# A first stage in another order: one block of a transformer on one NeuronCore

## What is computed

```
mod = silu(c) @ wmod                      # six sections: sa, ca, ga, sb, cb, gb for each batch
h   = layernorm(x) * (1 + ca) + sa
x   = x + ga * attn(h)                    # Mamba2-like: in_proj, causal conv of 4 taps, silu,
                                          # chunked scan with decays, gate silu(z), out_proj
h   = layernorm(x) * (1 + cb) + sb
x   = x + gb * (h @ (sign(w) * mean|w|).T + bias)
```

## Time and profile before

| | us |
|---|---|
| median of 3 executions | 655.74 (654.91 to 656.59) |
| the profiled execution | 658.04 |
| its span in the profile | 656.3 |
| TensorE busy | 612.0 (93%) |
| VectorE busy | 504.1 (77%) |
| ScalarE busy | 383.8 (58%) |
| GpSimd busy | 355.8 (54%) |

### The profile page before, as it was taken

One profiled execution on the slowest core, in us unless ns is written; L12 is line 12 of the kernel. 1 busy time (PEld: TensorE's weight loads), 2 busy tenths in 40 slices (PEclk: granted clock), 3 DMA queues, 4 the chain that ended last, 5 costly groups with the idle time before them and its releaser, 6 DMA issues.

```text
span 656.3 us, 21241 instructions
## 1 busy us (share of the span) xinstructions
PE 612.0 (93%) x8345; PEld 481.2 (73%) x8345; DVE 504.1 (77%) x928; ACT 383.8 (58%) x844; POOL 355.8 (54%) x411
## 2 busy tenths in 40 slices
PE   2788899999999999999999999999997999999995
PEld 1565677787787777878777787787875777888884
DVE  6797799978778787787977778778695566787756
ACT  2788555456465455655545655656664437566565
POOL 4776114347537355554543755547574657766642
PEclk9799999999999999999999999999999999999999
DMA  8734120613221221421222253231325735444411
GB/s 296 224 131 163 39 67 29 203 66 103 67 92 60 83 72 54 148 74 41 70 76 100 88 152 102 70 120 64 97 71 166 224 106 147 137 129 128 129 49 64
DMA packets 59866, 70.52 MB, mean 107 GB/s; under 512 B 13972, under 2 KB 33460, under 8 KB 59256
## 3 DMA queue, kind: packets, MB, share of 16 engines
q1 hardware_dynamic: 59768, 69.17, 33.0%
HBM read 54.45 MB, written 14.70 MB: 105 GB/s over the span
## 4 chain that ended last, share of the span: by engine, by line
PE 78%; DVE 7%; POOL 4%; issue 4%; ACT 3%; DMA 3%; SPq 1%; POOLq 0%; DVEq 0%; ACTq 0%
PE bank L1218 37%; PE bank L1985 12%; PE pair L1283 7%; PE bank L1227 4%; PE bank L2018 4%; PE pair L1256 3%; PE bank L1313 2%; PE bank L1236 2%; PE pair L1269 2%; DVE m_cv L1472 1%; POOL h_lo L435 1%; PE pair L1296 1%; DMA h_lo_place<-y_scratch 1%; PE bank L1245 1%; DVE p_xn L514 1%
## 5 line engine op out<-in xcount | busy, mean ns | idle before, releaser
L1472 DVE SCALAR_TENSOR_TENSOR m_cv<-bank,gpc,m_cv 128x511 f32<-128x511 f32 (+2 forms) x192 | 143.5, 748 | 36.0 <-ACT m_cv L1375 31.5
L1218 PE MATMUL bank<-h_hi,w_hi 128*128 128x512 f32 x384 | 163.2, 425 | 1.6 <-POOL h_lo L435 1.5
L1218 PE MATMUL bank<-h_hi,w_lo 128*128 128x512 f32 x384 | 152.0, 396 | 0.0
L1218 PE MATMUL bank<-h_lo,w_hi 128*128 128x512 f32 x384 | 151.4, 394 | 0.0
L1387 ACT ACTIVATE m_M<-bank 128x512 f32<-128x512 f32 x128 | 76.1, 594 | 65.9 <-PE bank L1227 64.1
L1375 ACT ACTIVATE m_cv<-bank,gpc 128x512 f32<-128x512 f32 x96 | 72.0, 750 | 72.6 <-PE bank L1218 72.1
L1614 POOL TENSOR_TENSOR m_S<-m_S,m_cd 128x128 f32<-128x128 f32 x96 | 40.2, 419 | 126.5 <-DVE m_S L1535 65.4
L1218 PEld LDWEIGHTS bank<-h_hi,w_hi 128*128 128x128 f32 x384 | 73.1, 190 | 22.1 <-issue 3.1
L1604 POOL TENSOR_TENSOR m_Xw<-m_Xp,wend 128x256 f32<-128x256 f32 x64 | 39.8, 622 | 85.4 <-ACT m_Xp L1395 85.4
L1218 PEld LDWEIGHTS bank<-h_hi,w_lo 128*128 128x128 f32 x384 | 72.5, 189 | 16.7
L1502 DVE TENSOR_TENSOR m_M<-m_M,pair 128x512 f32<-128x512 f32 x128 | 81.8, 680 | 0.3 <-issue 0.3
(11 more groups left out here) (179 smaller groups left out, 1228.9 us busy)
## 6 DMA issues: line engine op xcount, KB each, us to landing
m_ea<-ea_scratch SPq DMA_DIRECT2D x32, 256.0 KB
m_dd<-dd_scratch SPq DMA_DIRECT2D x32, 256.0 KB
y_scratch<-m_t SPq DMA_DIRECT2D x16, 512.0 KB, 3.4
h_lo_place<-y_scratch SPq DMA_DIRECT2D x16, 512.0 KB, 4.5
p_wm<-in_L_wmod_dram SPq DMA_DIRECT2D x6, 1024.0 KB, 6.7
m_wraw<-in_L_attn_in_proj_w_dram SPq DMA_DIRECT2D x18, 256.0 KB, 3.4
w_lo_place<-in_L_attn_input__dram SPq DMA_DIRECT2D x16, 256.0 KB, 4.8
out_dram<-t_o SPq DMA_DIRECT2D x16, 256.0 KB, 2.3
```

The source lines that it names most:

```text
L1218: ins = pe.matmul(A[k % 3][:, :], w[:, t, kc, :], h[:, n % NB, kc, :], start=(m == 0), stop=(m == 11))
L1472: ins = dve.scalar_tensor_tensor(out=cv[:, k % 3, lag:], in0=A[k % 3][:, 0:L - lag], scalar=s.gpc[:, gp, o:o + 1], in1=cv[:, k % 3, lag:], ...
```

## The change

It does four things.
- **Order in the first part.** VectorE does the product for silu(c), two `statistics`, the scaled copy for `mod`, two more `statistics`, and only then the memsets of the constant shapes. The two memsets of `wa_hi` and `wa_lo` go to GpSimd. GpSimd does `roots(0)` before `constant_shapes`, and `roots(3)` behind `low_part(6)`. TensorE does four turns before `early_sections` and the `wa` transposes; `late_sections(k)` each stand one project later, and `turn(12)` to `turn(15)` ahead of `late_sections(2)`. VectorE does `low_part(5)` and `low_part(7)` before `normalize(8)`, and `normalize(12)` to `normalize(15)` before `low_sums`. ScalarE does `decays` and `tanh(0)` ahead of `linear(2)`, and `copy_rows(1)` behind `linear(3)`.
- **Constant shapes by DMA.** The four copies of `stage` and `lstage` into `s.R` and `s.Lm` are issued by SyncE, ahead of the loads of x tiles 8 to 13, and no longer done by ScalarE.
- **dt_inputs(1, 0)** stands at the very end of TensorE's first part.
- **The last pair's step inputs.** `dt_inputs(1, 1)` stands at v = -2, sl = 3, in front of the second decay product; `softplus_inputs(1)` is cut in two, and its first two activations stand at v = -2, sl = 3, in front of ScalarE's other work of that slot; the gate transposes and gate rows stand in the same slot, and only their wait (`gates_turned`) at v = -1, sl = 0.

The diff, cut to its core:

```diff
@@ sync
         load_small()
+        sp.wait_ge(konst, 9)
+        for i in range(2):
+            sp.dma_start(s.R[:, i, :, :].bitcast(F32).rearrange("p q n -> p (q n)"), stage[:, :]).then_inc(kcopy, 16)
+            sp.dma_start(s.Lm[:, i, :, :].bitcast(F32).rearrange("p q n -> p (q n)"), lstage[:, :]).then_inc(kcopy, 16)
         for i in range(8, 14):
             load_x(i)
@@ gpsimd
+        pool.memset(wa_hi[:, :, :].bitcast(F32), 0.0).then_inc(zero_sc, 1)
+        pool.memset(wa_lo[:, :, :].bitcast(F32), 0.0).then_inc(zero_sc, 1)
...
+        roots(0)
         constant_shapes()
-        pool.wait_ge(konst, 9)
-        roots(0)
         chunk_starts()
...
         weights(1)
-        roots(3)
         low_part(4)
         low_part(6)
+        roots(3)
@@ vector
         dve.wait_ge(cond_step, 3)
+        for i in range(2):
+            statistics(dve, i)
         dve.wait_ge(zero_sc, 1)
...
-        for i in range(4):
+        for i in range(2, 4):
             statistics(dve, i)
+        for i, (first, _) in enumerate(LOG1P):
+            ins = dve.memset(root[:, i:i + 1], first)
+        ins.then_inc(a_root, 1)
+        dve.memset(stage[:, :], 0.0)
+        dve.memset(lstage[0:64, :], 0.0)
+        dve.memset(lstage[64:R_ALL, :], 1.0)
+        dve.memset(chunk_on[:, :], 1.0).then_inc(gpc_half, 1)
         for i in range(4):
             normalize(i)
...
-        normalize(8)
         low_part(5)
         low_part(7)
-        normalize(9)
-        normalize(10)
-        normalize(11)
+        for i in range(8, 12):
+            normalize(i)
...
         sums(dve, 0)
-        normalize(12)
+        for i in range(12, 16):
+            normalize(i)
         low_sums(dve, 0)
-        for i in range(13, 16):
-            normalize(i)
@@ scalar (first part)
         linear(1)
+        decays(act, 0)
+        tanh(0)
         linear(2)
-        decays(act, 0)
-        copy_rows(1)
         make_h(12)
         make_h(13)
-        tanh(0)
         make_h(14)
         make_h(15)
         tanh(1)
         linear(3)
+        copy_rows(1)
         tanh(2)
@@ gate_rows
-        softplus_inputs(act, 1)
         act.wait_ge(gate_pe, 1)
         act.activation(grow[:, :], MOD[0:2 * NB * KC, 0:P], ACT.Copy).then_inc(gate_ready, 1)
+        softplus_powers(act, 1)
         squares(act, 1, range(0, 2))
@@ tensor (first part)
         pe.wait_ge(cond_step, 4)
-        turn(0)
-        turn(1)
+        for i in range(4):
+            turn(i)
+        early_sections()
...
-        late_sections(0)
         project(1, 0)
         project(1, 1)
-        late_sections(1)
+        late_sections(0)
         project(2, 0)
         project(2, 1)
-        late_sections(2)
-        late_sections(3)
+        late_sections(1)
         for i in range(12, 16):
             turn(i)
-        dt_inputs(pe, 1, 0)
+        late_sections(2)
         project(3, 0)
         project(3, 1)
+        late_sections(3)
         pe.wait_ge(h_act, 14)
         end_turn(pe, 0)
+        dt_inputs(pe, 1, 0)
@@ tensor (main loop)
+                    if (v, sl) == (-2, 3):
+                        start.dt_inputs(pe, 1, 1)
                     if (v, sl) == (-1, 0):
-                        start.dt_inputs(pe, 1, 1)
-                        start.gate_turn(pe)
+                        start.gates_turned(pe)
...
                         turn_b(u)
+                    if (v, sl) == (-2, 3):
+                        start.gate_turn(pe)
@@ scalar (main loop)
-                    if (v, sl) == (-1, 0):
-                        start.gate_rows(act)
+                    if (v, sl) == (-2, 3):
+                        start.softplus_inputs(act, 1)
                     if slot >= 1 and piece_at(slot - 1) is not None:
                         weights(piece_at(slot - 1))
...
                         copy_b(u)
+                    if (v, sl) == (-2, 3):
+                        start.gate_rows(act)
```

More of the change, by code:

```diff
@@ L484, in vector @@
     def vector(dve, convolve, silu):
-        for i, (first, _) in enumerate(LOG1P):
-            ins = dve.memset(root[:, i:i + 1], first)
-        ins.then_inc(a_root, 1)
-        dve.memset(wa_hi[:, :, :].bitcast(F32), 0.0)
-        dve.memset(wa_lo[:, :, :].bitcast(F32), 0.0)
-        dve.memset(stage[:, :], 0.0)
-        dve.memset(lstage[0:64, :], 0.0)
-        dve.memset(lstage[64:R_ALL, :], 1.0)
-        dve.memset(chunk_on[:, :], 1.0).then_inc(gpc_half, 1)
         dve.wait_ge(d_c, 16)
@@ L522, in low_part @@
                               ALU.subtract).then_inc(h_lo[1], 1)
-        for i in range(4):
+        for i in range(2, 4):
             statistics(dve, i)
+        for i, (first, _) in enumerate(LOG1P):
[5 more added lines that the diff above has]
+        dve.memset(chunk_on[:, :], 1.0).then_inc(gpc_half, 1)
         for i in range(4):
             normalize(i)
-        dve.wait_ge(gpc_half, 1)
-        dve.wait_ge(wa_act, 1)
-        dve.tensor_tensor(wa_lo[:, :, 64:128], s.bank[5][:, 0:KC * NH].rearrange("p (k h) -> p k h", k=KC),
-                          wa_hi[:, :, 64:128].bitcast(F32), ALU.subtract).then_inc(wa_dve, 1)
         for i in range(4, 7):
@@ L535, in vector @@
         modulation(1)
+        dve.wait_ge(zero_sc, 3)
+        dve.wait_ge(wa_act, 1)
+        dve.tensor_tensor(wa_lo[:, :, 64:128], s.bank[5][:, 0:KC * NH].rearrange("p (k h) -> p k h", k=KC),
+                          wa_hi[:, :, 64:128].bitcast(F32), ALU.subtract).then_inc(wa_dve, 1)
         normalize(4)
@@ L659, in softplus_inputs, with softplus_powers @@
         act.activation(s.chain[:, pb, 1, :], DTB[:, :], ACT.Abs).then_inc(a_exp[pb], 1)
+    def softplus_powers(act, pb):
         act.wait_ge(a_exp[pb], 2)
@@ L703, in copy_rows @@
             act.activation(row[:, late, cols], DTB[:, cols], ACT.Copy).then_inc(sec_cp, 1)
-        act.wait_ge(konst, 9)
-        for i in range(2):
-            act.activation(s.R[:, i, :, :].rearrange("p q n -> p (q n)"), stage[:, :], ACT.Copy).then_inc(kcopy, 1)
-            act.activation(s.Lm[:, i, :, :].rearrange("p q n -> p (q n)"), lstage[:, :], ACT.Copy).then_inc(kcopy, 1)
+        copy_rows(0)
         act.wait_ge(wa_pe, 1)
+        act.wait_ge(zero_sc, 3)
         act.activation(wa_hi[:, :, 64:128], s.bank[5][:, 0:KC * NH].rearrange("p (k h) -> p k h", k=KC), ACT.Copy).then_inc(wa_act, 1)
-        copy_rows(0)
         for n in range(4):
@@ L720, in scalar @@
         softplus_inputs(act, 0)
+        softplus_powers(act, 0)
         squares(act, 0, range(5))
@@ L872, in tensor @@
         ins.then_inc(wa_pe, 1)
-        early_sections()
-        turn(2)
-        turn(3)
         turn_rows(pe, 0)
@@ L898, in tensor @@
             turn(i)
-        late_sections(0)
         project(1, 0)
         project(1, 1)
-        late_sections(1)
+        late_sections(0)
         project(2, 0)
         project(2, 1)
-        late_sections(2)
-        late_sections(3)
+        late_sections(1)
         for i in range(12, 16):
             turn(i)
-        dt_inputs(pe, 1, 0)
+        late_sections(2)
         project(3, 0)
         project(3, 1)
+        late_sections(3)
         pe.wait_ge(h_act, 14)
         end_turn(pe, 0)
+        dt_inputs(pe, 1, 0)
     start.sync, start.tensor, start.scalar, start.vector, start.gpsimd = sync, tensor, scalar, vector, gpsimd
     start.store_decays, start.store_skips, start.store_gates = store_decays, store_skips, store_gates
-    start.factors, start.finish_times, start.sums, start.low_sums, start.skips, start.squares = factors, finish_times, sums, low_sums, skips, squares
+    start.factors, start.finish_times, start.sums, start.low_sums, start.skips, start.squares, start.softplus_inputs = factors, finish_times, sums, low_sums, skips, squares, softplus_inputs
     start.decays, start.end_copy, start.end_turn = decays, end_copy, end_turn
-    start.gate_turn, start.gate_rows, start.gate_values, start.wait_low = gate_turn, gate_rows, gate_values, wait_low
+    start.gate_turn, start.gate_rows, start.gate_values, start.wait_low, start.gates_turned = gate_turn, gate_rows, gate_values, wait_low, gates_turned
     start.turn_sections, start.dt_inputs, start.gate_sizes, start.mlp_columns = turn_sections, dt_inputs, gate_sizes, mlp_columns
@@ L1132, in sync @@
             start.sync(sp)
-            sp.wait_ge(start.kcopy, 4)
+            sp.wait_ge(start.kcopy, 64)
             start.store_decays(sp, 0)
```

3 lines of the change are left out of this document (2 added, 1 removed).

## The result

| | us |
|---|---|
| kernel before, median | 655.71 (654.91 to 656.59) |
| kernel after, median | 665.34 (660.47 to 666.42) |
| ratio, with its 95% interval | 1.0121 (1.0088 to 1.0154) |
| profiled execution of after, its span | 660.47, 658.6 |

The change makes the kernel 9.6 us slower. The forecast was 660.6 and its range ended at 663.0. The profiled execution happens to be the quickest of the four; the other three took 665.3 to 666.4. So this profile can be laid beside the forecast step by step, but it holds only part of the loss; a second profile, shown with the first experiment, holds the rest.

A forecast was written before the change was run, and what follows sets the result against it. VectorE was taken as the bound from about 80 to 129 us. `convolve(4)` 6.5 us late less 1.2 slack gave 5.3; small gaps take about 0.3; +4.9 was taken: 655.74 + 4.9 = 660.6 us, range 654.8 to 663.0.

The forecast's parts named there:

- the deciding step: 61 to 91 us: softplus pair ahead of `linear(4)` makes `convolve(4)` 6.5 us late; 5.3 left at 86.14 after 1.2 slack.
- the middle: 49 to 63 us: four `normalize`s fill VectorE's wait, ending about 54.9; `silu(0)` ends at 60.7, 1.8 us sooner.
- the clock: `project(3)`, after TensorE idles from about 56.5 to 60.85 us: lower granted clock loses 1.7 us, bounds 0 and 3.0.
- `normalize` 0 to 3: VectorE's front: first starts about 10.4 us beside the `affine_select`s, fourth ends at 14.1; bounds 12.65 and 16.2.
- the term of the DMA copies: Four copies ahead of x8 to x13: 0 to 0.9 us of waiting for weight blocks, taken as 0.
- The issue: SyncE's four copy issues take 2.01 us; all later loads shift 2 to 2.4 us.
- The x tiles: x8 to x11 have one to two microseconds between landing and reading.
- The cover: TensorE's idle time of 1.53 us at 45.45 hides the weight-block wait; without it 0.9 us.
- the front order: 0 to 41 us: `factors(0)` comes at 40.8 instead of 41.21; bounds 39.3 and 42.2.
- Same: Rival, chance 0.17: TensorE's own order decides, `states(0)` +1.6 us, saved clock dip -1.7; 655.7 us.
- faster: Rival, chance 0.07: unhindered `normalize`s, clock stays up, VectorE's lateness within slack, `linear(4)` before 72.5; 652.1 us.
- Slower still: Rival, chance 0.08: TensorE, waiting for VectorE's mixes between 85 and 105 us, drops clock; another 1.7 to 3 us: 663.

The follow-up runs named there:

- the first experiment: The changed kernel run again without any edit, with a second profile and more executions (after_again): median 665.95 us, +8.9 over before.
- pair_behind: Changed kernel with the two softplus activations moved behind `linear(4)`, `exponent(0, 1)` and `copy_b` on ScalarE: median 661.38 us, +4.3 over before.
- slot_only: Kernel before with only the last pair's step inputs a slot earlier, softplus pair in front of `linear(4)`: median 659.02 us, +2.1.
- mid_only: Kernel before with only the change's middle (48 to 70 us), including `dt_inputs(1, 0)` at the end of the first part: median 659.99 us, +3.2.
- hole_slot: Kernel before with `skips(0)` moved into VectorE's wait for `decays`, and last pair's inputs a slot earlier, softplus pair behind `linear(4)`: 654.95 us, -2.0.
- dma_only: Kernel before with only the four constant-shape copies made DMAs ahead of x tile 8 instead of ScalarE activations: median 661.08 us, +4.2.
- copies_late: Changed kernel with the four constant-shape copies issued behind SyncE's loads of the first part: median 661.86 us, +4.9 over before.
- after_again: The changed kernel, no edit, profiled a second time with more executions: median 665.95 us, +8.9 over before.

## Why the prediction was right and where it failed

**Right: what bounds the kernel, and the deciding step.** VectorE's work between 80 and 129 us sets the time at which TensorE reaches its closed stretch. The forecast had `linear(4)` at 77.95 and `convolve(4)` 6.5 us late; measured 78.32 and 7.03. The reciprocal was to end at 84.5 and ends at 84.7. The lateness handed on was to be 5.3 us at the `convolve` of 86.14; it is 5.6 there and 5.6 at unit 6 in the first profile, and 5.3 to 5.5 at unit 6 in all three profiles with this order once the front is taken off. That this is the softplus pair and the queue behind `project(3)` is shown by pair_behind, slot_only and mid_only.

**Right: the middle and the clock.** `low_sums` starts at 55.70, where 54.9 was taken and 55.2 was the upper bound (0.65 us of it is that `factors(0)` came at 41.45 instead of 40.8); `silu(0)` starts at 60.74 and ends near 61.4 instead of 60.7. The four `normalize`s take 5.76 us, 1.44 each: each as long as one beside GpSimd in the row of before (1.45), and none was quicker. The granted clock of 60:66 is 0.72, which is the dip of the earlier trace rows moved: 1.7 us, as forecast, and `project(3)` takes 4.43 us where 4.7 was taken. TensorE had been idle for 4.09 us before it, and the clock came back to its upper level halfway through the twelve: the second product took 0.63 us, the eighth 0.40.

**Right in time, and in the rule beside it, for `normalize` 0 to 3.** They start at 10.16 and take 3.51 us, so they end at 13.7; 14.1 was taken. The Trainium skill, SBUF — State Buffer, section "Who interferes with whom", would have each of the last three blocked for a whole `affine_select`. The trace agrees: taken one by one, the four last 0.36, 1.38, 0.64 and 1.36 us, and the last three end about 0.3 us behind the first three selects, which take 1.15, 0.41 and 1.14 us (10.39 to 13.38). What did not come out is the end near 15.0 that the prediction worked out by it: the short select is among the three. Beside GpSimd's subtractions the trace agrees as well: 1.44 us each. The same section says that a VectorE instruction with one SBUF input outside the two-port modes does not contend; the reciprocal of hole_slot took 3.34 us in the midst of GpSimd's four subtractions (5.66 us from 49.65), and 3.35 in the kernel before at its old place.

**Wrong: the term of the DMA copies, 0 to 0.9 us of waiting, taken as 0.** This is the term that put the median outside the range. dma_only prices it at 4.2 us, and copies_late gives 3.9 back. The profiles show what stood behind it:
- The issue. Four issues were taken at 2.01 us, the price of four x tiles. These take 0.76 to 0.92 us each, 3.4 together, and the four x tiles behind them 2.47. The first raw weight block is issued at 27.43 instead of 24.14: 3.3 us later, where 2 to 2.4 were taken for all that follows.
- The x tiles. They were given one to two microseconds between landing and reading. VectorE waits 2.51 and 0.97 us for them in the first profile of after, and in dma_only they are what makes `dt_inputs(0, 1)` start late.
- The landing. In the kernel before a block lands 5.0 us after its issue, in after 6.1, in after_again 6.2 and up to 7.9, in dma_only 6.5. Nothing was taken for this. How much of it the copies cause is not shown, since it is 6.2 in mid_only, which has no such copy, and 6.8 in copies_late. The DMA engines moved 287 GB/s from 30 to 40 us before, 388 and 389 in the two profiles of after, and 353 in copies_late.
- The cover. The idle time of 1.53 us at 45.45 on TensorE was named as what hides a wait. It stands behind `dt_inputs(0, 1)`, and the waits come in front of it. The softplus chain and `factors(0)` hang on `dt_inputs(0, 1)`, so its delay was not TensorE's to absorb: it lay on the path from the start. The wait was judged by the engine that has it and not by who is queued behind it.
- The clock. A lower clock behind the waits was priced for `project(3)` only. It costs `dt_inputs(0, 1)` another 1.4 us in dma_only and 2.1 in after_again, and nothing in the first profile of after, where the products ran at 0.39 us.

By the medians of the single parts the sum is near the whole: copies ahead +4.2, slot +2.1, middle +3.2, front order -1.4, together +8.1 us; the whole measured +8.9 in a later series and +9.6 in the first. Each part's interval is 1.2 to 1.6 us wide to either side, so a difference of 1 us says nothing. The parts were measured at the kernel before; taken out of the change, the slot is worth 3.3 us (665.95 less 662.65).

**Half right: the front order.** The gain was put at 0.4 us (40.8 against 41.21) with a bound of 39.3. With the copies out of the way it is 1.6 in the profile and 1.4 in the median, whose interval just reaches no change. In the change itself nothing of it is left.

**The end.** The forecast handed 4.9 us on to the last instruction. That the quick execution of after took 660.47 us, next to the 660.6 forecast for the median, is chance: the forecast for the profiled execution was 662.9. In the first profile of after 5.6 at unit 6 are 4.3 at unit 58 and 2.3 at unit 63. Most other profiles lose about as much between units 58 and 63 (after_again 2.0, copies_late 1.5, dma_only 1.0), where TensorE idles in the kernel before as well. Why the first profile lost 1.3 us between units 6 and 58 was not tried.

**Rivals.** *Same* and *faster* are refuted by the row of 79.14 alone: `linear(4)` is far behind 72.5. *Slower still* (663) was nearest in time, and only the first half of its mechanism came about: TensorE waited 2.08 us at 87.71 and 1.25 at 95.72. Behind the first wait the clock did fall, to 0.64 from 88 to 90 us and 0.50 from 90 to 92. But this cost nothing: the lateness is 5.5 us at unit 1 and 5.5 at unit 10, since VectorE sets the time there.

## What to carry over

A DMA put ahead of others is to be priced by what the load behind it feeds: follow the first transfer that has little time to spare to its reader, and the reader's queue to whoever waits for that, before naming idle time elsewhere as cover. An activation moved in front of another on an in-order engine costs the full wait for its own input, even when it is needed soon; put it behind the one that feeds the bound engine. Idle time on the bound engine is best filled with work taken out of its own bound stretch (here a reciprocal, 3.3 us), and beside GpSimd's subtractions a `normalize` took 1.44 us instead of 0.56, while the reciprocal took no longer than elsewhere.
